# Row maxima from the rounded parts only: two 64-row score matmuls on the two halves of the array, one reduction over two banks

## What is computed

```
dim 128, 16 heads of 64, here b = 1, n = 2048
xn = x / norm(x) * sqrt(128) * (gamma + 1)
q, k, v = split(xn @ w_qkv);  q = q * 64 ** -0.5
sim  = q k^T                      # 2048 x 2048 for each head
attn = softmax(sim)               # over the keys
out  = (attn v, heads side by side) @ w_out
```

## Time and profile before

| | |
|---|---|
| median of 3 runs | 2309.75 us (2306.97 to 2312.76) |
| span of the profiled execution, first to last instruction | 2302.3 us |
| time of the profiled execution itself | not listed apart; the median lies 7.45 us above its span |
| PE busy | 2142.9 us, 93% |
| DVE busy | 1805.1 us, 78% |
| ACT busy | 1587.2 us, 69% |
| POOL busy | 1004.2 us, 44% |

### The profile page before, as it was taken

How to read it: one execution, slowest core, us unless ns; L and a number is a source line. 1 busy time by engine, 2 the same in 40 slices (tenths; PEclk the granted TensorE clock), 3 DMA queues, 4 the chain that set the end, 5 groups by cost and what they waited for, 6 DMA issues and landing times.

```text
span 2302.3 us, 32776 instructions
## 1 busy us (share of the span) xinstructions
PE 2142.9 (93%) x9032; PEld 1504.7 (65%) x9032; DVE 1805.1 (78%) x2535; ACT 1587.2 (69%) x1898; POOL 1004.2 (44%) x636
## 2 busy tenths in 40 slices
PE   6999459998779999999999999999999999999997
PEld 4777237776647666666766666666666667666654
DVE  5888867886588888887888788788888878888555
ACT  4666426664427877777787777777777787777873
POOL 1000100003025566565565656556565655656672
PEclk7999769998679999999999999999999999999998
DMA  3210003110000000000000000000000000000000
GB/s 115 63 49 19 0 0 75 43 30 15 1 3 1 12 1 14 3 10 10 7 12 4 12 3 10 15 1 12 5 11 3 10 15 1 12 2 10 11 1 19
DMA packets 25125, 36.59 MB, mean 16 GB/s; under 512 B 11807, under 2 KB 14239, under 8 KB 23711
## 3 DMA queue, kind: packets, MB, share of 16 engines
q1 hardware_dynamic: 24958, 34.56, 5.8%
HBM read 32.99 MB, written 1.43 MB: 15 GB/s over the span
## 4 chain that ended last, share of the span: by engine, by line
PE 73%; DVE 13%; issue 7%; ACT 4%; POOL 2%; DVEq 0%; DMA 0%; ACTq 0%; POOLq 0%
PE ps L478 14%; PE ps L480 13%; PE ps L479 13%; PE ps L586 8%; PE ps L608 8%; PE ps L609 8%; DVE m_part L1219 2%; PE ps L460 2%; DVE p_l L1249 2%; POOL p_l L380 1%; ACT p_raw L926 1%; DVE m_part L1331 1%; DVE kb L1207 1%; PE ps L613 1%; PE ps L453 1%
## 5 line engine op out<-in xcount | busy, mean ns | idle before, releaser
L380 POOL TENSOR_TENSOR p_l<-p_raw,p_h 128x512 fp32r<-128x512 f32 (+1 forms) x512 | 836.9, 1635 | 651.3 <-ACT p_h L930 645.4
L1219 DVE TENSOR_REDUCE m_part<-ps 128x1 f32<-128x512 f32 x960 | 643.3, 685 | 191.0 <-PE ps L586 186.1
L926 ACT ACTIVATE p_raw<-ps 128x1024 f32<-128x1024 f32 x512 | 524.9, 1025 | 308.6 <-PE ps L609 283.6
L930 ACT ACTIVATE p_h<-p_raw 128x1024 fp32r<-128x1024 f32 x512 | 543.0, 1061 | 27.5
L1249 DVE TENSOR_TENSOR p_l<-p_raw,p_h 128x512 fp32r<-128x512 f32 x384 | 431.0, 1123 | 63.9 <-ACT p_h L930 49.8
L608 PE MATMUL ps<-qa,ka 128*128 128x512 f32 x1024 | 418.3, 408 | 7.4 <-DMA qb<-m_t 7.4
L478 PE MATMUL ps<-p_h,v_l 128*65 128x512 f32 x1024 | 404.4, 395 | 7.2 <-DVE p_l L1249 6.1
L609 PE MATMUL ps<-qb,kb 65*128 65x512 f32 x1024 | 407.5, 398 | 0.0
L479 PE MATMUL ps<-p_h,v_h 128*65 128x512 f32 x1024 | 402.6, 393 | 0.0
L480 PE MATMUL ps<-p_l,v_h 128*65 128x512 f32 x1024 | 402.4, 393 | 0.0
L586 PE MATMUL ps<-ka,qa 128*128 128x512 f32 x960 | 381.9, 405 | 8.0 <-DVE m_part L1219 5.6
(11 more groups left out here) (177 smaller groups left out, 2730.8 us busy)
## 6 DMA issues: line engine op xcount, KB each, us to landing
big<-g_scratch SPq DMA_DIRECT2D x64, 256.0 KB, 3.2
xnp<-r_scratch SPq DMA_DIRECT2D x15, 512.0 KB, 4.8
big<-in_w1T SPq DMA_DIRECT2D x1, 2048.0 KB, 9.0
big<-in_w2T SPq DMA_DIRECT2D x1, 2048.0 KB, 13.5
x<-in_xT SPq DMA_DIRECT2D x4, 256.0 KB, 3.6
qk_raw<-in_w_qkv SPq DMA_DIRECT2D x32, 32.0 KB, 1.9
out_xT<-x SPq DMA_DIRECT2D x4, 256.0 KB, 2.0
wv_raw<-in_w_qkv SPq DMA_DIRECT2D x8, 64.0 KB, 1.9
```

The lines of the kernel that those rows point to most:

```text
L380: nc.gpsimd.tensor_tensor(p_l[:, g % 4, tiles, :], p_raw[:, g % 4, tiles, :], p_h[:, g % 4, tiles, :].bitcast(fp32), ALU.subtract).then_in ...
L926: af(p_raw[:, g % 4, :, :], ps[:, 2 * (g % 2):2 * (g % 2) + 2, :], ACT.Exp).then_inc(exp_done, 1)
L930: af(p_h[:, g % 4, :, :], p_raw[:, g % 4, :, :], ACT.Copy).then_inc(ph_done, 1)
L1219: nc.vector.tensor_reduce(m_part[:, ds(c, 1), it:it + 1].rearrange("p a t -> p (a t)"), ps[:, 4 + it % 2, :], AX.X, ALU.max).then_inc(s_ma ...
```

## The change

Score tiles are done in pairs. The even tile multiplies the high parts on rows 0 to 63 (`qa` and `kb`) into bank 4, the odd tile the high parts on rows 64 to 127 (`qa` and `ka`) into bank 5; the product with the low part of k is left out of the maxima (the maxima are only subtracted in the exponent, and the sums are made with the same ones). One wait stands ahead of a pair: for the reductions of all tiles before it. One DVE instruction reduces both banks to two columns. A group that had two or three tiles has one or two pairs, the first behind `scores_t`, the second behind `values`. The first pair of a window also waits for `kb_done`.

```
-MAXIMA_TILES = ((0, 2, 2, 3, 2, 2, 3, 2), (2,) * 8, (2,) * 8, (3, 3, 3, 2, 2, 2, 1, 0))
+MAXIMA_PAIRS = ((0, 1, 1, 2, 1, 1, 1, 1), (1,) * 8, (1,) * 8, (2, 1, 1, 1, 1, 1, 1, 0))
...
-            def score_tile(head, par, c, it):
-
-                if it < 2:
-                    pe.wait_ge(s_max, PRIME + NC * NT * head + NT * c)
-                else:
-                    pe.wait_ge(s_max, PRIME + NC * NT * head + NT * c + it - 1)
-                mm(ps[:, 4 + it % 2, :], qa[par][:, it * 128:it * 128 + 128], ka[par][:, ds(c * CH, CH)],
-                   start=True, stop=True).then_inc(s_ps, 1)
+            def score_pair(head, par, c, ip):
+
+                pe.wait_ge(s_max, PRIME + NC * NT * head + NT * c + 2 * ip)
+                even, odd = 2 * ip * 128, 2 * ip * 128 + 128
+                mm(ps[:, 4, :], qa[par][0:DH, even:even + 128], kb[par][0:DH, ds(c * CH, CH)],
+                   start=True, stop=True)
+                mm(ps[:, 5, :], qa[par][DH:128, odd:odd + 128], ka[par][DH:128, ds(c * CH, CH)],
+                   start=True, stop=True).then_inc(s_ps, 2)
...
-                def next_score_tile():
-                    it = next(tiles)
-                    if first and it % TPC == 0:
-                        pe.wait_ge(lo_done, 8 * (head + 1) + 2 * (it // TPC) + 2)
-                        pe.wait_ge(hi_done, 12 * (head + 1) + 3 * (it // TPC) + 3)
-                    if first and it == 1:
+                pairs = iter(range(NT // 2))
+
+                def next_score_pair():
+                    ip = next(pairs)
+                    if first and ip == 0:
                         pe.wait_ge(hi_done, 12 * (head + 2))
                         pe.wait_ge(lo_done, 8 * (head + 2))
-                    score_tile(head + 1, 1 - par, c, it)
+                        pe.wait_ge(kb_done, NC * (head + 2))
+                    score_pair(head + 1, 1 - par, c, ip)
...
                     scores_t(par, c, g)
-                    if with_next and first and g == 0:
-                        before = 0
-                    else:
-                        before = min(1, MAXIMA_TILES[c][g])
-                    if with_next:
-                        for _ in range(before):
-                            next_score_tile()
+                    if with_next and MAXIMA_PAIRS[c][g] > 0:
+                        next_score_pair()
...
                         values(head, par, c, g - PV_LAG)
-                    if with_next:
-                        for _ in range(MAXIMA_TILES[c][g] - before):
-                            next_score_tile()
+                    if with_next and MAXIMA_PAIRS[c][g] > 1:
+                        next_score_pair()
...
-            def maximum(head, c, it):
-                dve.wait_ge(s_ps, NC * NT * head + NT * c + it + 1)
-                nc.vector.tensor_reduce(m_part[:, ds(c, 1), it:it + 1].rearrange("p a t -> p (a t)"),
-                                        ps[:, 4 + it % 2, :], AX.X, ALU.max).then_inc(s_max, 1)
+            def maximum(head, c, ip):
+                dve.wait_ge(s_ps, NC * NT * head + NT * c + 2 * ip + 2)
+                nc.vector.tensor_reduce(m_part[:, ds(c, 1), 2 * ip:2 * ip + 2].rearrange("p a t -> p (a t)"),
+                                        ps[:, 4:6, :], AX.X, ALU.max).then_inc(s_max, 2)
```

More of the change, by code:

```diff
@@ L637, in spare_free @@
                     read(c, g)
-                tiles = iter(range(NT))
-                def next_score_tile():
-                    it = next(tiles)
-                    if first and it % TPC == 0:
-                        pe.wait_ge(lo_done, 8 * (head + 1) + 2 * (it // TPC) + 2)
-                        pe.wait_ge(hi_done, 12 * (head + 1) + 3 * (it // TPC) + 3)
-                    if first and it == 1:
+                pairs = iter(range(NT // 2))
+                def next_score_pair():
+                    ip = next(pairs)
+                    if first and ip == 0:
                         pe.wait_ge(hi_done, 12 * (head + 2))
                         pe.wait_ge(lo_done, 8 * (head + 2))
-                    score_tile(head + 1, 1 - par, c, it)
+                        pe.wait_ge(kb_done, NC * (head + 2))
+                    score_pair(head + 1, 1 - par, c, ip)
                 for g in range(GROUPS):
@@ L1280, in main_chunk @@
                     if with_next:
-                        for _ in range(MAXIMA_TILES[c][g]):
-                            maximum(head + 1, c, next(tiles))
+                        for _ in range(MAXIMA_PAIRS[c][g]):
+                            maximum(head + 1, c, next(pairs))
                         if (c, g) == (NC - 1, GROUPS - 2):
```

## The result

The changed kernel is slower: 2349.44 us median of 4 runs (2347.91 to 2354.87) against 2311.07 us (2306.97 to 2312.76), ratio 1.0172 with a 95% interval of 1.0155 to 1.0189. That is +38 us in the medians and 43.7 us in the spans of the two profiled executions. The direction was forecast; the size was not: +105 us were forecast, +38 came. 2349.44 us lies inside the stated range (2340 to 2495), near its low end, which stood for both halves starting at once and the whole credit for shorter waits.

A forecast was written before the change was run, and what follows sets the result against it. PE's distances between matmul starts were taken as the bound. +125 us on PE for 480 pairs less 20 us of waits gave +105 on the 2302.3 us span, 2407, plus 7.45 to the median: 2415 us, range 2340 to 2495.

The forecast's parts named there:

- both halves starting at once: PE, low end: a pair's two matmuls take 0.23 us, making +0.16 us a pair, +77 us in all.
- the whole credit for shorter waits: PE's waits for reductions: at most 50 us saved, taken in full for the low end of the range.
- the sum on PE: Each of 480 pairs: 0.33 + 0.39 - 0.46 = +0.26 us, +125 us in all.
- The two matmuls: A pair's halves on PE: 0.33 us, from 0.23 plus 0.10 for the second weight load; ends 0.23 and 0.46.
- The border: PE's way into and out of a 64-row pair among full matmuls: 0.39 us a pair, bounds 0 and 0.39.
- The reduction of 1024 elements: DVE: one reduction over both banks takes 1218 ns, saving 152 ns a pair, 73 us of DVE in all.
- Low part, 1123 ns: DVE in a plain group: 1123 ns plus a 1218 ns reduction, 2.34 us, covered by about 3.0 us between pairs.
- The credit of 20 us: PE's waits for reductions: middle credit of 32 us less 12 us at groups with two pairs, -20 us net.
- no overlap (0.22): PE pairs: the border costs 0.39 us but the halves don't overlap, +167 us, 2477 us; chance 0.22.
- A 64-row matmul without a border (0.11): PE pairs: halves overlap with no border, -0.13 us a pair, 2228 us, or 2180 with both at once; chance 0.11.
- No change on PE (0.05): PE pairs: no border and no overlap, only the waits change, 2290 to 2310 us; chance 0.05.
- The wait for the pair before (0.04): Forecast plus pairs waiting for their predecessor's reduction, 0.3 us each, +144 us more, 2559 us; chance 0.04.

The follow-up runs named there:

- full tiles and the short reduction: Changed kernel with both tiles of a pair as full 128-row matmuls and a reduction reading only 64 of 512 columns per bank, scores scaled by 1/16: 2276.17 us.
- single tile: Kernel before with 64-row score tiles one at a time, alternating lower and upper half, one 512-element reduction each: 2592.68 us, ratio 1.1224.
- full tiles with one reduction: Changed kernel with both tiles of a pair as full 128-row matmuls, the single wait and single reduction over both banks kept: 2334.03 us, 1.0103.
- both tiles on one half: Changed kernel with both tiles of a pair on rows 0 to 63, so they can't run side by side: 2450.78 us, 1.0621.
- short reductions: Changed kernel with reductions reading 64 of 512 columns per bank, scores scaled by 1/16: 2329.86 us with 64-row halves, 2276.17 us with full 128-row tiles.

## Why the prediction was wrong in size

The times add up. The run with full tiles and the short reduction (2276.17 us) has next to no waits for reductions. Above it lie the kernel before by 31.5 us (2307.65 on the same chip), which I count as waits, and the changed kernel, taken by its ratio, by 53.7 us for its pairs and (1.0172 - 1.0091) x 2309 = 19 us of waits. Together +53.7 + 19 - 31.5 = +41, measured 1.7% or 40.

**The step that failed** is the sum on PE, +0.26 us a pair: it is 0.112. The mechanism was right and the term mis-sized, in two parts:

- The two matmuls: I took 0.33 us, the middle of three values, because the rows gave 0.10 between two weight loads in a row. They take 0.23: weights and matmuls of the two halves start at the same time. The 0.10 came from two loads that both use rows 0 to 64 of the array; loads for different halves don't hold each other up. 0.10 x 480 = 48 us, the larger part. The lower bound was the right value.
- The border: 0.39 us from the one-row fp32 matmul. Here it is 0.23 + 0.11 = 0.34, or 0.36 by the rows of the single tile. Most of the difference lies behind the pair, where 449 of 480 times 65 columns of weights are loaded and not 128 (0.28 against 0.34). 0.05 x 480 = 24 us.

That the time still lies in the stated range is partly luck. Even with both halves at once the range had +77 us on PE, and 53.7 came; the low end of 2340 stood below 2349.44 only because it took the whole credit of 50 us, of which some 13 came.

The Trainium skill, TensorE: Matmul & The Clock Gate, Part 3, The mechanism, has row tiles start about 4 ns apart. The trace agrees: both are listed at 1353.47. By that sentence the sum would have been +0.16 us a pair. The Trainium skill, TensorEngine Tiling (Array Packing), Key Properties, has the engine drain when the mode changes, and has different tiles load and multiply in parallel. The single tiles (+283 us) agree with the first, the two halves (0.00 us apart) with the second.

Step by step:

- PE's start distances are the time of this stage: right. 42 of the 43.7 us in the traces are in this stretch, and a plain group of 12 matmuls takes 12 x 0.23 us before, and 0.12 more after.
- No weights are loaded ahead over a border, at 64 rows as at one row: right.
- The reduction of 1024 elements, 1218 ns: 1222 measured. But the 73 us that it was to save DVE were wrong, since 152 ns a pair took two reductions as 2 x 685: two in a row take 1.29 us. Against the kernel before, where most stand apart, it is 57 us.
- Low part, 1123 ns, for the 2.34 us of DVE work between two pairs: 839 in the changed kernel, so there was more cover than I counted.
- The credit of 20 us: about the size (31.5 - 19 = 13), but that was luck. The joined reduction brings nothing that can be measured (2353.02 against 2349.44 us), and with full tiles the pairing costs 24 us. What hides waits in the changed kernel is that PE itself got slower: the pair costs 53.7 us by itself but only 15 us on top of the full tiles with one reduction. That PE's listed waits would fall below 50 us was wrong, they rose to 80.8.
- `kb_done` costs nothing: right, 2.5 us of cover (the copy ends at 1286.13, the pair starts at 1288.62).
- Windows of 107 us: 1524 / 15 = 102.
- 7.45 us from span to median: 3.4 here, 4 us of the forecast that had nothing to do with the change.
- 1.18 us from the matmul before a pair to the second one after it: 1.04.

The rivals: no overlap (0.22) would have needed the time of the run with both tiles on one half, which is 101 us longer. A 64-row matmul without a border (0.11) fell with the single tiles. No change on PE (0.05) fell with the short reductions. The wait for the pair before (0.04) is there, but small: the loads of 124 of the 480 pairs list the reduction as what they waited for, and all waits together are 19 us in the changed kernel, against the 144 that I gave this rival.

## What to carry to other kernels

Splitting the array pays per border, not per matmul: two half-array matmuls at once save 0.23 us, and getting from full-array matmuls to them and back costs 0.34 us, so a single pair between full matmuls loses 0.11 us. With the same numbers two pairs behind one border would come out at 0.34 - 0.46 = -0.12 us; that is an estimate, it needs four free banks, which this kernel hasn't, and it wasn't tried. When two reductions are joined into one, look at what becomes of the buffers that took turns: here the 30 us that joining saves DVE weren't on the path, and with full tiles the pairing cost 24 us. And when a price is taken over from rows of another shape, take its parts apart first: the load that holds up the next matmul depends on its columns, and here the second load was held up where it shared rows with the first, and not on the other half.

## What the runs showed of the hardware

- The border hangs on one row: 65 rows of 128 (0 to 64) run in step with full matmuls (0.24 us, weights ahead), 64 rows don't (0.33 us, weights with the matmul).
- Two 64-row matmuls on different halves start within 0.01 us of each other; a lone one takes as long from its start to that of the next full one (0.43 us) as the two together.
- Between two 64-row matmuls on the same half there is no border: the second weights are loaded under the first matmul, 0.11 us after the first ones (1401.98 and 1401.87).
- The step behind a border grows with the columns of the weights loaded there: 0.28 us to the next matmul for 65, 0.34 for 128 (medians of 449 and 23 pairs in the changed kernel).
- Two reductions of 512 elements right behind each other overlap on DVE: 1.29 us for both, where one is listed with 0.685.
